# Attention's weighted values computed the other way round on TensorE

## The reference

```python
scores = jnp.einsum('bhqd,bhkd->bhqk', Q, K) / math.sqrt(D_K)      # D_K = 16, 16 heads
attn = jax.nn.softmax(scores, axis=-1)                              # over 64 context tokens
out = jnp.einsum('bhqk,bhkd->bhqd', attn, V)
out = out.transpose(0, 2, 1, 3).reshape(b, sd, d)
return out @ Wo + bo                                                # then x = layernorm(x + ...)
```

## Time and profile before

| | us |
|---|---|
| median of 3 runs | 363.29 |
| lowest, highest | 362.89, 364.42 |
| the profiled execution | 363.08 |
| its span in the trace | 361.3 |
| PE busy in the span | 268.4 (74%) |
| VectorE (DVE) busy | 192.3 (53%) |
| ScalarE (ACT) busy | 146.2 (40%) |
| GpSimd (POOL) busy | 150.2 (42%) |

### The profile page before, as it was taken

The page is one execution under the profiler, slowest core; times in us unless marked ns, Lnnn a source line. Parts: engine busy times, 40 slices in busy tenths (PEclk is TensorE's granted clock), DMA queues, the critical chain, the costliest instruction groups (busy, mean ns, idle before and its releaser), DMA issues.

```text
span 361.3 us, 4666 instructions
## 1 busy us (share of the span) xinstructions
PE 268.4 (74%) x1499; PEld 206.3 (57%) x1499; DVE 192.3 (53%) x602; ACT 146.2 (40%) x264; POOL 150.2 (42%) x192
## 2 busy tenths in 40 slices
PE   2989999897877899999984100235999999999300
PEld 2855565554545669999973000233778878788200
DVE  2345645848856438746773777821553261561054
ACT  3444255142576326464222703001891581920015
POOL 5490215462542204454221590037823296235423
PEclk9999999999999869999996555555999999999755
DMA  7921000007172706320001996014342044432566
GB/s 202 260 19 31 1 2 1 1 0 173 43 179 53 167 0 135 84 45 3 1 2 21 362 409 222 1 27 109 105 155 20 11 108 106 75 61 31 58 229 235
DMA packets 29951, 33.87 MB, mean 94 GB/s; under 512 B 8207, under 2 KB 22248, under 8 KB 29672
## 3 DMA queue, kind: packets, MB, share of 16 engines
q1 hardware_dynamic: 26504, 29.25, 28.2%
q0 software_dynamic: 3072, 4.26, 7.4%
q10 hardware_dynamic: 352, 0.07, 0.1%
HBM read 16.99 MB, written 8.45 MB: 70 GB/s over the span
## 4 chain that ended last, share of the span: by engine, by line
PE 55%; DVE 16%; DMA 8%; ACT 8%; issue 6%; POOL 5%; SPq 1%; ACTq 0%; DVEq 0%; POOLq 0%
PE bank L981 12%; PE bank L1211 8%; PE bank L1161 4%; DMA summed_rows<-OUT,idx 4%; PE bank L1353 4%; DVE junk L1645 4%; PE bank L1060 3%; PE bank L1198 2%; PE bank L1144 2%; POOL summed_rows L748 2%; PE bank L1243 2%; DMA Y<-summed_rows 2%; PE bank L1174 2%; DMA X<-in_x 2%; POOL rstd L685 2%
## 5 line engine op out<-in xcount | busy, mean ns | idle before, releaser
L684 POOL TENSOR_SCALAR var_eps<-mean_var 128x1 f32<-128x1 f32 (+1 forms) x36 | 8.3, 230 | 82.5 <-DVE mean_var L1525 82.1
L748 POOL DMA_INDIRECT summed_rows<-OUT,idx x16 | 26.3, 1646 | 34.0 <-DVE OUT L1722 21.5
L1211 PEld LDWEIGHTS bank<-VB,PT 128*128 128x128 f32 x256 | 34.0, 199 | 1.4
L1211 PE MATMUL bank<-VB,PT 128*128 128x34 f32 x256 | 33.4, 276 | 0.0
L1353 PE MATMUL bank<-WDH,MH 128*128 128x256 f32 x96 | 30.3, 315 | 0.0
L1737 DVE TENSOR_TENSOR ML<-bank,MH 128x512 fp32r<-128x512 f32 (+1 forms) x24 | 16.3, 687 | 25.5 <-ACT MH L954 25.4
L737 POOL DMA_INDIRECT XG<-routed_rows,idx x16 | 15.5, 966 | 27.7 <-DVE idx L1714 23.2
L1532 DVE TENSOR_REDUCE NMF<-bank 128x8 f32<-128x512 f32 x32 | 21.8, 682 | 9.6 <-PE bank L1174 9.5
L1353 PE MATMUL bank<-WDL,MH 128*128 128x256 f32 x96 | 26.9, 280 | 0.0
L1353 PE MATMUL bank<-WDH,ML 128*128 128x256 f32 x96 | 26.9, 280 | 0.0
L950 ACT ACTIVATE bank<-bank,b_up_c 128x512 f32<-128x512 f32 (+1 forms) x24 | 15.6, 650 | 25.5 <-PE bank L981 25.0
(11 more groups left out here) (279 smaller groups left out, 744.4 us busy)
## 6 DMA issues: line engine op xcount, KB each, us to landing
WDR<-in_L_ffn_W_down SPq DMA_DIRECT2D x8, 640.0 KB
QS<-QH SPq DMA_DIRECT2D x32, 128.0 KB, 3.2
WUR<-in_L_ffn_W_up SPq DMA_DIRECT2D x4, 682.0 KB, 6.2
routed_rows<-X SPq DMA_DIRECT2D x2, 1056.0 KB, 11.0
X<-in_x SPq DMA_DIRECT2D x4, 512.0 KB, 6.2
QS<-QL SPq DMA_DIRECT2D x16, 128.0 KB, 2.8
summed_rows<-X SPq DMA_DIRECT2D x2, 1024.0 KB, 10.4
Y<-summed_rows SPq DMA_DIRECT2D x8, 256.0 KB, 5.4
```

What stands on the lines that cost most here:

```text
L748: pool.indirect_dma_start(summed, bass.IndirectOffsetOnAxis(ap=idx[:, 2 * e + h:2 * e + h + 1].bitcast(U32), axis=0), OUT[:, (2 * e + h) % ...
L1211: last = pe.matmul(o[:, j * 34:(j + 1) * 34], PT[m % 2][:, j, s * P:(s + 1) * P], VB[:, m // 2, j].rearrange("p h d -> p (h d)"), start=Tr ...
```

## The change

The product is turned round. For a block m and a half c of the heads (four pairs), the four pairs' values (VB, 128x32, without the column of ones) are the weights and the 512 columns of PT move; pair q of the half writes the 32 partitions from 32q on of bank 7. A second group of four does the same with `head_ones` (ones for the pair's own head) as weights into bank 0, so that every row holds its head's sum. One reciprocal of 128x512 and one product of 128x512 give ATT with the features on partitions, a block at a time; no transpose, no split. Wo stays in f32, and the output product is one f32 product per half. There are 8 such parts (m, c); `pv_part` puts them in every second unit, 9 to 23: numerators in the unit's first half, denominators in its second. z2, x2t and lg come one unit earlier. ScalarE, before it overwrites PT for block m, waits for the denominators of block m-2.

```diff
-    LAG = {"z1": -5, "mx": 2, "nmt": 6, "sc": 7, "pv": 11, "att": 12, "z2": 13, "x2t": 15, "lg": 16}
+    LAG = {"z1": -5, "mx": 2, "nmt": 6, "sc": 7, "z2": 12, "x2t": 14, "lg": 15}
...
-        WO = [place(n, [P, KC, D], F32R) for n in ("WOH", "WOL")]
+        WO = place("WO", [P, KC, D], F32)
...
-        VB = place("VB", [P, B, PR, 2, DK + 1], F32)
-        ATT = place("ATT", [P, TPB, D], F32)
-        ATH = place("ATH", [P, 2, KC, P], F32R)
-        ATL = place("ATL", [P, 2, KC, P], F32R)
+        VB = place("VB", [P, B, PR, 2, DK], F32)
+        head_ones = place("head_ones", [P, 2, DK], F32)
+        ATT = place("ATT", [P, 2, KC, BLK], F32)
...
-        REC = place("REC", [P, 2, HD], F32)
+        REC = place("REC", [P, KC, BLK], F32)
...
+        def pv_part(g):
+
+            m, c = (g - LAG["sc"] - 2) // TPB, (g - LAG["sc"] - 2) % TPB // 2
+            return (m, c) if 0 <= m < NB and (g - LAG["sc"]) % 2 == 0 else None
...
-                if half == 0 and live(g, "pv"):
-                    product(("pv", g - LAG["pv"]), 7)
+                if pv_part(g) is not None:
+                    product((("num", "den")[half],) + pv_part(g), (7, 0)[half])
...
-            whole(WO, wo_s, wo_in)
...
-                if j == 0 and m >= 2:
-                    wait_filled(act, ("pv", TPB * (m - 1) - 1))
+                if j % TPB == 0 and m >= 2:
+                    wait_filled(act, ("den", m - 2, j // TPB))
...
-                    act.activation(ATH[:, t % 2], bank_of(("att", t))[:, 0:D], ACT.Copy).then_inc(ath_made, 1)
...
-            def weighted(t, half):
-
-                m, s = t // TPB, t % TPB
-                o = turn(("pv", t)) if half == 0 else bank_of(("pv", t))
...
-                    last = pe.matmul(o[:, j * 34:(j + 1) * 34], PT[m % 2][:, j, s * P:(s + 1) * P],
-                                     VB[:, m // 2, j].rearrange("p h d -> p (h d)"), start=True, stop=True)
...
+            def weighted(m, c, half):
+
+                what = ("num", "den")[half]
+                o = turn((what, m, c))
...
+                for q in range(TPB):
+                    j = TPB * c + q
+                    if half == 0:
+                        wait_moved(pe, ("sc", m, j))
+                    w = (VB[:, m // 2, j], head_ones[:])[half]
+                    last = pe.matmul(o[32 * q:32 * q + 32, :], w.rearrange("p h d -> p (h d)"), PT[m % 2][:, j, :],
+                                     start=True, stop=True)
+                last.then_inc(sem_filled((what, m, c)), 1)
...
-            def attention_transposed(t):
...
-                split_matmuls(o[:, 0:D], [
-                    ((ATH[:, t % 2, c], ATL[:, t % 2, c]), both(WO, ALLP, c, ALLP)) for c in range(KC)
-                ]).then_inc(sem_filled(("z2", t)), 1)
+                for c in range(KC):
+                    if s == 0:
+                        wait_moved(pe, ("num", m, c))
+                    last = pe.matmul(o[:, 0:D], ATT[:, m % 2, c, s * P:(s + 1) * P], WO[:, c, :],
+                                     start=(c == 0), stop=(c == KC - 1))
+                last.then_inc(sem_filled(("z2", t)), 1)
...
-                if i == 3:
-                    low(WO, wo_s, 3)
...
+            def inverse_sums(m, c):
+                wait_filled(dve, ("den", m, c))
+                dve.reciprocal(REC[:, c], bank_of(("den", m, c))[:]).then_inc(sem_moved(("den", m, c)), 1)
+
+            def attended(m, c):
+
+                wait_moved(dve, ("den", m, c))
+                if m >= 2:
+                    wait_filled(dve, ("z2", TPB * (m - 1) - 1))
+                dve.tensor_tensor(ATT[:, m % 2, c], bank_of(("num", m, c))[:], REC[:, c], ALU.mult)\
+                    .then_inc(sem_moved(("num", m, c)), 1)
```

More of the change, by code:

```diff
@@ L367, in decoder_block @@
                     product(("q", block_of(g - c, "q"), c), 4 + c)
-            if live(g, "att"):
-                product(("att", g - LAG["att"]), 0)
             if live(g, "z2"):
@@ L547, in _ @@
                     sp.wait_ge(km_made, 4)
-                    sp.wait_ge(w_lo, 3)
+                    sp.wait_ge(w_lo, 2)
                 for q in range(PR // KC):
@@ L643, in _ @@
             pool.wait_ge(vb_init, 1)
-            link(pool.memset(VB[0:SE, :, :, 0, DK:DK + 1], 1.0))
-            pool.memset(VB[SE:P, :, :, 1, DK:DK + 1], 1.0).then_inc(vb_init, 1)
+            link(pool.memset(head_ones[:], 0.0))
+            link(pool.memset(head_ones[0:SE, 0], 1.0))
+            pool.memset(head_ones[SE:P, 1], 1.0).then_inc(vb_init, 1)
             pool.wait_ge(vb_init, 2)
@@ L876, in _ @@
                             act.wait_ge(km_made, 4)
-                            act.wait_ge(w_lo, 3)
+                            act.wait_ge(w_lo, 2)
                         elif n >= 2:
@@ L1199, in scores @@
                     .then_inc(sem_filled(("sc", m, j)), 1)
-            def weighted(t, half):
-                m, s = t // TPB, t % TPB
-                o = turn(("pv", t)) if half == 0 else bank_of(("pv", t))
[L1205 to L1208, removed]
-                    if s == 0:
-                        wait_moved(pe, ("sc", m, j))
-                    last = pe.matmul(o[:, j * 34:(j + 1) * 34], PT[m % 2][:, j, s * P:(s + 1) * P],
-                                     VB[:, m // 2, j].rearrange("p h d -> p (h d)"), start=True, stop=True)
-                if half == 1:
-                    last.then_inc(sem_filled(("pv", t)), 1)
@@ L1216, in attention_transposed @@
-            def attention_transposed(t):
[L1217 to L1225, removed]
-                split_matmuls(o[:, 0:D], [
-                    ((ATH[:, t % 2, c], ATL[:, t % 2, c]), both(WO, ALLP, c, ALLP)) for c in range(KC)
-                ]).then_inc(sem_filled(("z2", t)), 1)
+            def weighted(m, c, half):
+                what = ("num", "den")[half]
+                o = turn((what, m, c))
+                if (m, c, half) == (0, 0, 0):
+                    pe.wait_ge(vb_made, 2)
+                    pe.wait_ge(vb_init, 2)
+                    wait_moved(pe, ("v", 1))
+                for q in range(TPB):
[6 more added lines that the diff above has]
+                last.then_inc(sem_filled((what, m, c)), 1)
@@ L1264, in _ @@
                         maxima_transposed(block_of(g, "nmt"))
-                    if live(g, "pv"):
-                        weighted(g - LAG["pv"], half)
+                    if pv_part(g) is not None:
+                        weighted(*pv_part(g), half)
                 for c in range(KC):
@@ L1551, in maxima_low @@
                     .then_inc(nm_made, 1)
[L1553 to L1567, removed]
+            def inverse_sums(m, c):
[7 more added lines that the diff above has]
+                    .then_inc(sem_moved(("num", m, c)), 1)
             for g in UNITS:
-                z1, mx, pv, z2 = [g - LAG[k] for k in ("z1", "mx", "pv", "z2")]
+                z1, mx, z2 = [g - LAG[k] for k in ("z1", "mx", "z2")]
                 if live(g, "z1"):
@@ L1594, in _ @@
                     maxima_high(mx)
-                if live(g, "pv"):
-                    inverse_sums(pv)
                 if live(g, "mx"):
                     maxima_low(mx)
-                if live(g, "pv"):
-                    attended(pv)
+                if pv_part(g) is not None:
+                    inverse_sums(*pv_part(g))
+                    attended(*pv_part(g))
                 for c in range(KC):
@@ L1612, in _ @@
                                       ALU.subtract, ALU.mult).then_inc(ln2_out_dve, 1)
[L1613 to L1618, removed]
                 if live(g, "z2"):
```

16 lines of the change are left out of this document (4 added, 12 removed).

## The result

The changed kernel takes 391.47 us (median of 4 runs, 389.20 to 393.12), the kernel before 363.74 in the same comparison: 1.0724 times as long, 95% interval 1.0676 to 1.0773. The forecast was 395 us, slower. The profiled execution took 389.20 us, its span is 387.4 (before 361.3). The routing's first instruction, the mark of the prediction's sum, starts at 219.28 us (before 196.51): 22.8 of the span's 26.1 us are gone by then.

A forecast was written before the change was run, and what follows sets the result against it. TensorE was taken to bound the kernel now; after the change, a loop through VectorE's wide reciprocal. From 363.1 us, +24.4 for the loop and +8 for the clock gave 395 us, range 371 to 421 for 8 in 10.

The forecast's parts named there:

- N: TensorE time of one group of four 32-column f32 matmuls, taken as 2.15 us since only neighbours of different groups overlap.
- Rival (a): TensorE's four column groups run abreast, a group taking 0.86 us: kernel at 376 us, chance 0.21.
- The reciprocal: VectorE's new 128x512 reciprocal per part, priced per element at 4.0 us, with 0.79 and 8.2 as alternatives.
- The clock: PE idles in the new loop and the granted clock falls: 1.7 us a fall, five of eight, +8 us.
- the prediction's own sum: Time to the routing's first instruction, 186.5 + 16N, so 220.9 us instead of 196.51.
- the loop's work by itself: Later start of the routing from the VectorE and TensorE loop, without the clock: +24.4 us.
- the prediction's cycles: Times between successive parts in units 9 to 23, each 7.1 to 10.9 us plus 2N, summing to 57.0 + 14N.
- The loop through bank 6: PE's next output product waits for the X sum behind the reciprocal: 12.3 us per two units, against 7.6.
- PE's own sum: TensorE's work per pair of units, 3.94 + 2N: 8.2 us against 7.6, a gain only below N = 1.8.
- The unit count: Output product, X2 and logits come one unit earlier, so one unit fewer, included in the +24.4 us.
- bank 0's waits: x1t of unit 12 and nmt (unit 14) wait until the reciprocal frees bank 0; x1t's wait 4.1 us.
- the things at nothing: WO's splitting gone (at most 0.7 us gained), two GpSimd memsets (0 to 0.5 lost), ScalarE copies gone; counted as nothing.

The follow-up runs named there:

- e1: The changed kernel with the 128x512 reciprocal replaced by a plain copy, the division left out: 357.73 us, ratio 0.9847 to the kernel before.
- e3: The changed kernel with filler matmuls into an idle bank ahead of the output product from unit 18 on: 384.41 us, ratio 1.0569 to the kernel before.
- e2: The changed kernel with all four matmuls of a group in one column group, three quarters of the bank uncomputed: 426.14 us, ratio 1.1699.
- e10: The changed kernel with 256 of the 512 columns inverted and the other 256 only copied: 363.95 us, ratio 1.0120 to the kernel before.
- e12: The changed kernel with output products of odd units from 19 on in bank 2 instead of bank 6: 388.61 us, ratio 1.0661.
- e5: The changed kernel with reciprocal and ATT moved behind the X sum and statistics in VectorE's order: 401.97 us, ratio 1.1023.
- e4: The kernel before plus eight 128x512 reciprocals of constants that nobody reads, in odd units 11 to 25: 396.53 us, ratio 1.0856.
- e11: The kernel before plus eight half-width reciprocals of 128x256: 362.44 to 366.16 us in three runs, 391.14 and 400.04 in two; ratio 1.0118 from the three.
- e6: The changed kernel with sums transposed, inverted on 32 columns a part, spread by ScalarE and turned back: 374.04 us, ratio 1.0241.

## Why the prediction was right, and where it was not

The direction, the place and the cause held: VectorE's reciprocal of a bank closes a loop with TensorE (e1), and the clock falls in that loop and costs time of its own (e3). That the time came within 4 us of the forecast is luck: two errors met, and the main term of the sum was not the one that cost the time. At the mark the forecast stood at 228.9 us (220.9 and the clock's 8), the trace says 219.28.

- **N, wrong.** "If only neighbours of different groups overlap" was the step that failed. It made N 2.15; it is 0.99 to 1.04 at the high clock (1.00 in e1, 3.55 in one column group, e2). 16 x 1.14 = 18 us too much. Rival (a) had it: N = 0.86, nearly. The Trainium skill (TensorEngine Tiling, "Key Properties") lets tiles run independently, by its "Theoretical Speedup" up to 4 times as fast; here four column groups give 3.55 times one, near that, and my count of program order was the worse guide.
- **The reciprocal, a little too long.** 4.0 us against 3.35, 5 us over eight. The rows of 16, 32, 256 and 512 columns (256 ns, 353, 1754, 3352) lie on one line of 6.2 ns an element and 0.16 us; I had put 6.5 on top of an ordinary pass that is already in the rate.
- **The clock, far too small.** With N = 1.01 and 3.35 us the prediction's own sum at the high clock is 186.5 - 5.2 + 16.2 = 197.5, and 0.9 less for unit 9's start (106.18 instead of 107.09). The kernel before stands at 196.51, so the loop's work by itself, +24.4 us in the forecast, comes to nothing (VectorE's own line, as in rival (a), adds less than 1.5), and the remaining 22.7 us stand against the 8 I gave the clock. I had counted 1.7 us for five of eight falls and nothing for the tail; even in the kernel before the fall of the earlier trace rows lasts longer than the 3.5 us that I assumed, from 127.5 to 134.25 us:

```profile
127.50:134.25 6.75, 6.75 (x20) 4.38 (x19) 1.75 (x6) 0.74 (x2) 0.00 (x0) 0.50 0.00 0
```

In the tail behind the last reciprocal the kernel after takes 25.1 us where the sum gives 20.5, three units at 3.9 us and one at 3.2 instead of 2.5; that is the clock's, since e3 takes 20.9 us for it at 1.00.

The seven distances between the eight reciprocals come to 84.5 us, where the prediction's cycles give 66.6 with the measured costs: 17.9 more. Not all of that is the clock. In e10, with the clock at 0.98, the distances come to 65.0 us, where the same cycles give 57.6 with the 2.06 us that stand in the reciprocal's place: 7.4 more. By these two the clock's share of the 22.7 us is an estimated 15 to 23, nearly twice the 8 or more, and up to 7 lie in paths that my cycles leave out, such as VectorE's maxima between the X sum and the next part. No run separates them further. The stretch of e10:

```profile
100.00:174.25 74.25, 62.53 (x321) 32.77 (x321) 52.42 (x119) 31.77 (x61) 26.19 (x41) 0.98 0.34 76
```

- **The loop through bank 6, half right.** It exists (7.7 us of waits, e12), but it is one of several: e5 took the reciprocal out of its old place in it and ended 10 us slower. The prediction priced the wait by the bank; the chain from unit 15 to 17 runs through VectorE's program order instead, and e12, which frees the bank behind the last three parts, leaves most of the loss.
- **PE's own sum, right in kind.** Below N = 1.8 TensorE gains; N is 1.0, and e1 is 1.5% faster than the kernel before. The idea of the change is good on TensorE and is undone on VectorE.
- **The unit count, bank 0's waits and the things at nothing** came out nearly as written: x1t and nmt waited 3.6 and 2.1 us, nmt in another unit, and PE is busy 85.6 and 85.7 of the first 100 us.

So the cause was right and the time near by luck, with 23 us too much in two terms and some 15 too little in the clock and what else the cycles left out. With N at four abreast and the same 8 us for the clock the forecast is rival (a), 376, 15 us too low; with the measured reciprocal as well it would have been about 371.

Open: what lets the clock stay down while PE is 93 and 97% busy (e4, e11) but holds it up in the traced run of e6, where PE is busy 28.17 of the 30 us from 150 on at 1.00. They differ in what PE runs (e4 and e11 have 34-column products behind full weight loads, e6 has 512-column ones), but that can't be all: the kernel before, with the same 34-column products, stays at 1.00 from 137.5 to 170 us. No run changed that alone.

## What to carry to other kernels

When a product is turned so that a per-row value must be copied over rows, count the elementwise work behind it by free-size columns: 16 divisions a token had become 256, and only VectorE's column count mattered. Price a reciprocal by its elements, not as one more pass. And read a stretch in which PE is dense as two things, work and the clock that the work keeps up: a stall put into it was paid here once as a wait and again as slow work afterwards (e1: 31.9 us of time for 21.3 us of VectorE; e3: 6 us back by work that does nothing). Moving the stall to another place (e5) was no cure, while halving it (e10) gave back more than half.

## What the runs showed that I had not expected

- Four f32 matmuls of 32 weight columns in four column groups take 1.00 us for 8 MATMULs of 512 columns; the same in one column group takes 3.55. The pairs of one product overlap with the next product's although they are issued in order.
- Filler matmuls that cost 0.96 us a unit shortened a unit from 3.9 to 3.2 us (e3).
- One kernel ran in 362 to 366 us or in 391 to 400 (e11); in the run of 391 its clock was at 0.54 in 40 us of 97% busy PE. What parts the two outcomes stays open.
